# Sampling weights made by halves, one shift moved behind the samples, a later table load, and one neighbour tap instead of two

## Chip, core and metric

One NeuronCore of one Trainium2 chip runs the whole program; there is one launch and no other core takes part. The metric is device microseconds of one execution. Busy times below are per engine: PE is TensorE, PEld its weight loads, DVE is VectorE, ACT is ScalarE, POOL is GpSimd, SP is SyncE.

## What is computed

The input is 8 images of 32 channels and 16x16 pixels. Three layers follow one another: a deformable-attention block, plain self-attention over the 256 tokens of each image, and a routed feed-forward layer. The change lies in the first:

```
q   = wq x                                  (1x1 convolution of the normalised image)
off = w_off gelu(norm(depthwise 5x5, stride 4, of q))      -> 16 key points per image and group
pos = reference points + tanh(off[0:2]) / 4
xs  = bilinear sample of x at pos, times sigmoid(off[2])
k,v = wk xs, wv xs
bias[m, n] = bilinear sample of the table rpe at (query m - pos n)
out = softmax(q k * scale + bias) v,  x += wo out
```

There are G = 2 groups of 16 channels, each with 2 heads, and 16 keys a group and image. The hat of a distance d is max(0, 1 - |d|); a bilinear sample is a sum over all pixels or rows weighted by hats.

## The kernel before

Every engine has an instruction list written out by hand, in order, with explicit semaphores; no planner or scheduler moves anything. `link(...)` issues an instruction and makes its own engine wait until it has finished. Most tiles have 128 partitions: image times channel of a group, key of all images (8 x 16), or half of the 256 pixels.

What concerns the change, in the order of the data:

- **Hats of the samples.** ACT forms `a_smp` (|pixel - position|, slots 0 and 1 for the rows of the two halves of the image, slot 2 for the columns; L547) and `hat_smp` from all three slots in one instruction (L558). POOL multiplies slots 0 and 2, then 1 and 2, to `w_smp[:, 0]` and `w_smp[:, 1]` (L486).
- **Samples.** PE multiplies the transposed image by `w_smp` into `xs_ps` (L744), two halves for each of two groups, summed in PSUM. DVE multiplies by the sigmoid written as 1 + tanh(half) to `xs` (L1116). PE projects `xs` to keys (L754, `project(0)`), ACT copies them for each head to `kv` (L571).
- **Table of the bias.** PE interpolates rows of the table (L733) to `row_ps[g]`: 128 keys, 32 rows (16 image rows x 2 heads), 21 columns of which 17 or so are wanted, starting at a whole column shift of 0 to 4 that differs by key. DVE moves the columns in place with predicated copies (L1101): by 2 where `over[..., 1]`, by 1 where `over[..., 3]`, by 1 where `odd`; three copies for each group. What is left is a fraction of a column, and three products by `tap` (L390), with weights `tap_prev`, `tap_next`, `tap_here`: `left`, `right`, `here`. Group 0's are made by POOL from `win`, a copy in SBUF that ACT makes (L566); group 1's by DVE from PSUM.
- **Logits.** PE transposes each product, adding in PSUM, to `lg_ps` (L761, `turn_on`), and adds q k (L783), for half h = 0 and then 1 of the query pixels. `logits_done` lets DVE take the maximum (L1130) and subtract it (L1131); ACT makes the exponents (L577, L581). PE meanwhile projects values (L754 again), adds the image (L797) and multiplies by wo (L805); then it transposes the probabilities (L816).
- **Fillers.** `keep_busy` (L680) has PE multiply zeros, a fixed number of times, where it would otherwise stand: 20 ahead of L744, 8 ahead of the key projection.
- **Table of functions.** ACT loads the set with Ln and Exp (L511) behind `half_tanh` (L562) and ahead of `win`.

Of the kernel before, what the change touches and what calls it, by code (L numbers as in the profile page):

```python
# [14 lines left out]
P = 128  # L15
B, C = 8, 32
IMG = 16
# [113 lines left out]
def build(nc, x_in, consts_in, weights_in, w1_in, w2_in, out):  # L131
    with ExitStack() as ctx:
# [9 lines left out]
        def bank(n, cols=512):  # L142
            return ps[:, 512 * n:512 * n + cols]
# [143 lines left out]

        qpad_ps = [bank(2 + g, PADIMG * PADIMG).rearrange("p (y x) -> p y x", y=PADIMG) for g in range(G)]
# [134 lines left out]
        def _(pool):  # L423
            steps = [0]

            def link(ins):
                steps[0] += 1
                ins.then_inc(pool_step, 1)
                pool.wait_ge(pool_step, steps[0])
# [52 lines left out]
            nc.gpsimd.tensor_scalar(tap_next[:, :, :], dist[:, :, :], 0.0, None, ALU.max)  # L482
            link(nc.gpsimd.tensor_scalar(tap_prev[:, :, :], dist[:, :, :], -1.0, 0.0, ALU.mult, ALU.max))
            pool.wait_ge(hat_smp_ready, 1)
            for h in range(NHALF):
                nc.gpsimd.tensor_tensor(w_smp[:, h], hat_smp[:, h], hat_smp[:, 2], ALU.mult).then_inc(w_smp_ready, 1)  # L486
# [18 lines left out]
        def _(act):  # L505
# [38 lines left out]
            def distance(a, k, axis, place):  # L544

                act.wait_ge(points_ready, axis + 1)
                return nc.scalar.activation(a[:, k], points[:, axis], ACT.Abs, bias=const(place)[:, k:k + 1],  # L547
                                            scale=-1.0)
# [5 lines left out]
            for k in range(3):  # L554
                distance(a_smp, k, 0 if k < NHALF else 1, "at_pixel").then_inc(a_smp_ready, 1)

            act.wait_ge(a_smp_ready, 3)
            nc.scalar.activation(hat_smp[:, :, :], a_smp[:, :, :], ACT.Relu, bias=1.0, scale=-1.0).then_inc(  # L558
                hat_smp_ready, 1)
# [3 lines left out]
            load_table(LN_EXP_SET)  # L563

            act.wait_ge(shifts_done, 1)
            nc.scalar.activation(win[:, :, :], row_ps[0][:, :, 0:IMG + 1], ACT.Copy).then_inc(win_copied, 1)  # L566
# [103 lines left out]
        def _(pe):  # L670
            mm = nc.tensor.matmul

            def nx_rows(nx):

                return slice(nx * P // NK, (nx + 1) * P // NK)
# [53 lines left out]
            for g in range(G):  # L729
                for yq in range(4):  # L730
                    pe.wait_ge(hat_rel_ready, yq + 1)
                    for nx, least in enumerate(table_columns()[0]):
                        last = mm(row_ps[g][nx_rows(nx), 8 * yq:8 * yq + 8, 0:WIN],  # L733
                                  minus_hat_rel[:, yq, g * P + nx:(g + 1) * P:NK],
                                  rpe_blk[:, g].rearrange("p k (h c) -> p (k h) c", h=HG)[:, :, least:least + WIN],
                                  start=True, stop=True)
                last.then_inc(rows_done, 1)
# [3 lines left out]
            pe.wait_ge(w_smp_ready, 2)  # L741
            for g in range(G):
                for h in range(NHALF):
                    last = mm(xs_ps[:, g], xn_tok[:, h, g], w_smp[:, h, g * P:(g + 1) * P],  # L744
                              start=(h == 0), stop=(h == NHALF - 1))
# [23 lines left out]
            pe.wait_ge(txh_ready, 1)  # L769
            pe.wait_ge(part_ready[0], 1)  # L770
# [6 lines left out]
            pe.wait_ge(part_ready[1], 1)  # L777
            for h in range(NHALF):
                turn_on(left, 1, h)
            pe.wait_ge(k_ready, HG)  # L780
            for h in range(NHALF):
                for g in range(G):
                    mm(lg_ps[:, h, g].rearrange("p t k j -> p (t k j)"), q_sb[:, g, h * P:(h + 1) * P],  # L783
                       kv[:, 0, g].rearrange("p t k j -> p (t k j)"), start=False, stop=False, skip_group_check=True)
                pe.wait_ge(part_ready[1], 2)
                turn_on(right, 1, h)
                pe.wait_ge(part_ready[0], 3)
                turn_on(here, 0, h)
                pe.wait_ge(part_ready[1], 3)
                turn_on(here, 1, h).then_inc(logits_done, 1)  # L790
# [243 lines left out]
        def _(dve):  # L1034
# [64 lines left out]
            def shifted(g, width, mask, by):  # L1099

                return nc.vector.copy_predicated(  # L1101
                    row_ps[g][:, :, 0:width], mask.bitcast(U32).unsqueeze(2).to_broadcast([P, IMG * HG, width]),
                    row_ps[g][:, :, by:by + width])
# [9 lines left out]
            link(shifted(1, IMG + 2, over[:, 1, 3:4], 1))  # L1113
# [3 lines left out]
                in1=xs_ps.rearrange("p g n -> p (g n)"), op0=ALU.add, op1=ALU.mult).then_inc(xs_ready, 1)  # L1117
            shifted(1, IMG + 1, odd[:, 1:2], 1).then_inc(shifts_done, 1)
# [3 lines left out]
            dve.wait_ge(left_edge_zeroed, 1)  # L1122
            tap(nc.vector, left, 1, row_ps[1], -1, tap_prev, 1).then_inc(part_ready[1], 1)
            tap(nc.vector, right, 1, row_ps[1], 1, tap_next).then_inc(part_ready[1], 1)
            tap(nc.vector, here, 1, row_ps[1], 0, tap_here).then_inc(part_ready[1], 1)
# [165 lines left out]
```

## Time and profile before

| | |
|---|---|
| runs | 60.14, 60.37, 61.9 us; median 60.37 |
| profiled execution | 59.97 us, its span 58.0 us |
| PE busy | 50.6 us (87% of the span), fillers included |
| PEld, DVE, ACT, POOL busy | 41.8, 36.9, 29.9, 18.4 us |
| granted TensorE clock | 1.0 in all 40 slices of the span |
| chain that ended last | PE 57%, DVE 14%, POOL 8%, ACT 7%, issue 5%, DMA 4% |

The span runs from the first to the last instruction; 1.97 us of the profiled execution lie around it. The rows of a timeline give start, length, engine, line, operation, output and inputs, and in brackets how long the engine stood before and for whom. Times of neighbours on one engine overlap a little, because an instruction starts before the one ahead has drained.

### The profile page before, as it was taken

What the parts mean: (1) busy time and instruction counts of PE and PEld (TensorE: products, weight loads), DVE (VectorE), ACT (ScalarE), POOL (GpSimd) and SP (SyncE); (2) the same over time, 40 slices, a digit from 0 to 9 for tenths busy, and PEclk for the clock granted to TensorE, in tenths of its full rate; (3) what the DMA queues carried; (4) which work ended last, traced back from release to release, by engine and by line L of the source; (5) the groups of instructions that cost most, each with busy time, mean ns of one, the idle gap of its engine ahead of it and who ended that gap; (6) DMA issues with size and microseconds to landing.
All of it is one profiled execution on the core that took longest, in us unless ns stands there. A gap on an engine that the chain in (4) does not pass through costs nothing.

```text
span 58.0 us, 1496 instructions
## 1 busy us (share of the span) xinstructions
PE 50.6 (87%) x603; PEld 41.8 (72%) x603; DVE 36.9 (64%) x95; ACT 29.9 (52%) x66; POOL 18.4 (32%) x41
## 2 busy tenths in 40 slices
PE   3996996999699699999999999979999998979720
PEld 3995894985388579899898986726688675867500
DVE  3478399775659989449994046739267866785320
ACT  0802052787999903104744785197984639801020
POOL 6130089995878899910060000000000000000000
PEclk9999999999999999999999999999999999999999
DMA  0889931110000000000000000000000000000013
GB/s 0 206 183 263 253 105 46 57 41 11 0 0 0 0 11 0 0 0 0 0 0 0 0 0 17 6 0 0 0 0 11 0 0 0 0 0 0 0 44 136
DMA packets 3926, 2.02 MB, mean 35 GB/s; under 512 B 2640, under 2 KB 3792, under 8 KB 3920
## 3 DMA queue, kind: packets, MB, share of 16 engines
q1 hardware_dynamic: 1424, 1.37, 8.1%
q10 hardware_dynamic: 2496, 0.57, 4.7%
q8 instruction: 4, 0.07, 0.5%
q14 instruction: 2, 0.02, 0.1%
HBM read 1.67 MB, written 0.26 MB: 33 GB/s over the span
## 4 chain that ended last, share of the span: by engine, by line
PE 57%; DVE 14%; POOL 8%; ACT 7%; issue 5%; DMA 4%; DVEq 0%; ACTq 0%
PE ps L761 5%; DMA x_sb<-x_rows 4%; PE ps L805 4%; PE ps L754 4%; PE ps L826 4%; PE ps L680 3%; PE ps L884 3%; PE ps L867 3%; PE ps L783 3%; DVE taps L1070 3%; POOL w_smp L486 2%; PE ps L889 2%; ACT e_tok L621 2%; DVE off L1072 2%; PE ps L1030 2%
## 5 line engine op out<-in xcount | busy, mean ns | idle before, releaser
L680 PE MATMUL ps<-zeros 128*128 128x128 bf16 x145 | 11.2, 237 | 1.0 <-DVE zeros L1047 1.0
L680 PEld LDWEIGHTS ps<-zeros 128*128 128x128 bf16 x145 | 10.1, 107 | 1.5 <-DVE zeros L1047 1.0
L511 ACT ACT_TABLE_LOAD x4 | 5.1, 1283 | 1.7 <-PEq L1284 1.6
L621 ACT ACTIVATE e_tok<-ps,cst 128x512 f32<-128x512 f32 (+1 forms) x6 | 4.5, 828 | 1.5 <-PE ps L867 1.5
L1101 DVE COPY_PREDICATED ps<-over,ps 128x608 f32<-128x608 uint32 (+1 forms) x4 | 3.1, 777 | 0.8 <-PE ps L733 0.7
L733 PE MATMUL ps<-rpe_blk,minus_hat_rel 128*32 128x168 f32 x64 | 2.8, 316 | 0.5 <-DVE minus_hat_rel L1097 0.5
L571 ACT ACTIVATE kv<-ps,cst 128x256 f32<-128x256 f32 x4 | 1.7, 472 | 2.8 <-PE ps L754 2.8
L733 PEld LDWEIGHTS ps<-rpe_blk,minus_hat_rel 128*32 128x32 f32 x64 | 2.0, 142 | 1.3 <-issue 0.9
L884 PE MATMUL ps<-e_tok,t 128*32 128x128 f32 (+1 forms) x48 | 2.8, 310 | 0.0
L1148 DVE TENSOR_REDUCE ln_ss<-ln_sq 128x8 f32<-128x264 f32 x2 | 0.9, 428 | 3.0 <-ACT ln_sq L601 3.0
L867 PE MATMUL ps<-t_t 32*128 32x256 f32 x32 | 2.3, 398 | 0.4 <-ACT e_tok L621 0.4
L439 POOL TENSOR_TENSOR wblk<-wts,cst 128x256 f32<-128x256 f32 x3 | 1.9, 628 | 2.2 <-DMA wts<-weights 2.2
L398 POOL TENSOR_TENSOR d_prob<-d_exp,d_rec 128x512 f32<-128x512 f32 x1 | 1.1, 1058 | 4.6 <-DVE d_rec L1137 4.6
L1130 DVE TENSOR_REDUCE d_max<-ps 128x32 f32<-128x512 f32 x2 | 1.4, 692 | 1.7 <-PE ps L761 1.6
L577 ACT ACTIVATE d_exp<-d_sub 128x512 f32<-128x512 f32 x1 | 0.6, 629 | 3.4 <-DVE d_sub L1131 3.4
L690 PE MATMUL ps<-xn,wblk 128*128 128x256 f32 x8 | 2.0, 388 | 0.5 <-DVE xn L1063 0.5
L835 PE MATMUL ps<-prob_t,vo 128*128 128x256 f32 x8 | 2.3, 393 | 0.0
L754 PE MATMUL ps<-xs,wblk 128*128 128x128 f32 x16 | 2.2, 281 | 0.1
L527 ACT ACTIVATE xn_tok<-ps 128x512 f32<-128x512 f32 x1 | 0.6, 598 | 3.2 <-PE ps L697 3.2
L867 PEld LDWEIGHTS ps<-t_t 32*128 32x128 f32 x32 | 1.5, 184 | 0.9 <-issue 0.9
L754 PEld LDWEIGHTS ps<-xs,wblk 128*128 128x128 f32 x16 | 1.9, 191 | 0.3 <-DVE xs L1116 0.3
L1070 DVE TENSOR_TENSOR taps<-ps,wts 128x100 f32<-128x100 f32 x8 | 1.5, 253 | 1.0 <-PE ps L690 1.0
(189 smaller groups left out, 129.9 us busy)
## 6 DMA issues: line engine op xcount, KB each, us to landing
w_sb<-weight ACTq DMA_DIRECT2D x1, 256.0 KB, 6.0
w_sb<-weight SPq DMA_DIRECT2D x1, 256.0 KB, 5.2
x_nat<-x_rows SPq DMA_DIRECT2D x8, 32.0 KB
wts<-weights SPq DMA_DIRECT2D x1, 192.5 KB, 4.5
cst<-shape_consts SPq DMA_DIRECT2D x1, 192.0 KB, 4.1
x_sb<-x_rows SPq DMA_DIRECT2D x1, 128.0 KB, 2.4
x_sb<-x_rows ACTq DMA_DIRECT2D x1, 128.0 KB, 2.6
cst<-shape_consts SPq DMA_DIRECT2D x1, 128.0 KB, 5.0
```

Source lines behind the costliest of these rows:

```text
L511: nc.scalar.add_instruction(mybir.InstLoadActFuncSet(name=nc.get_next_instruction_name(), act_func_set_id=functions, ins=[], outs=[]))
L621: return nc.scalar.activation(dst, scores, ACT.Exp, bias=const("bound"))
L680: mm(bank(n_bank, P), zeros[:, :], zeros[:, :], start=True, stop=True)
L733: last = mm(row_ps[g][nx_rows(nx), 8 * yq:8 * yq + 8, 0:WIN], minus_hat_rel[:, yq, g * P + nx:(g + 1) * P:NK], rpe_blk[:, g].rearrange("p ...
L754: last = mm(kv_ps[w][:, g], wblk[:, 1 + w, gi, g].rearrange("p b o -> p (b o)"), xs[:, gi], start=(gi == 0), stop=(gi == G - 1))
L761: last = mm(lg_ps[:, h, g, :, hh], part[:, g, hh, 8 * h:8 * h + 8].rearrange("p y x -> p (y x)"), back_to_n[:, :].rearrange("p (t j) -> p ...
L805: last = mm(outputs[:, g, t], kv[:, 1, g, t].rearrange("p k j -> p (k j)"), blk[:, g, B4 * t:B4 * t + B4].rearrange("p b o -> p (b o)"), s ...
L826: last = mm(att_ps[h][:, P * t:P * t + P], prob_t[:, h, g, t], vo_c[:, g, t], start=False, stop=(g == G - 1), skip_group_check=True)
L867: return mm(scores, t1_t[rows, b // B4, h * P:(h + 1) * P], t1_t[rows, b // B4, :], start=start, stop=True, skip_group_check=True)
L884: return mm(out[C * (b % B4):C * (b % B4) + C], t1[:, h, b], e_tok[:, b, h, queries], start=start, stop=stop, skip_group_check=True)
L1070: last = tt(taps[:, g, i].rearrange("p j (a b) -> p j a b", a=KS), conv_view(g, i), dw, ALU.mult)
L1101: return nc.vector.copy_predicated(row_ps[g][:, :, 0:width], mask.bitcast(U32).unsqueeze(2).to_broadcast([P, IMG * HG, width]), row_ps[g][ ...
```

## The change

1. ACT makes the hats one by one: distance of the columns, of half 0's rows, their two hats, then distance and hat of half 1. POOL makes `w_smp` half by half as the hats come, ahead of `tap_prev` instead of behind it. PE waits for one half at a time and takes half 0 of both groups first.
2. DVE makes `xs` between the first and the second shift of group 1, not between the second and third.
3. ACT copies `win` before it loads the set with Exp.
4. The table rows stand one column further right in `row_ps` (column 0 is free); `table_ps` is the view from column 1. For group 1, DVE makes `here` first; then a predicated copy overwrites each column by the one two further right where `tap_next` is not zero, so that the column holds the right neighbour for one sign of the fraction and the left for the other; then one product with `tap_both` (the sum of the two weights, of which one is zero) takes the place of `left` and `right`. PE has four transposes fewer, and adds q k before group 1's parts.

```diff
--- before.py
+++ after.py
@@ -285,6 +285,7 @@
         sq_ps = [bank(n, M) for n in (4, 2)]
         y_ps = [bank(n, M) for n in (1, 5)]
 
+        table_ps = [row_ps[g][:, :, 1:] for g in range(G)]
         qpad_ps = [bank(2 + g, PADIMG * PADIMG).rearrange("p (y x) -> p y x", y=PADIMG) for g in range(G)]
         q_ps = [qpad_ps[g][:, PAD:PAD + IMG, PAD:PAD + IMG] for g in range(G)]
         att_ps = [bank(2 + h, B * C) for h in range(NHALF)]
@@ -480,10 +481,10 @@
             link(nc.gpsimd.tensor_tensor(dist[:, :, :], frac[:, :].unsqueeze(2).to_broadcast([P, G, IMG]),
                                          const("frac_x").unsqueeze(1).to_broadcast([P, G, IMG]), ALU.subtract))
             nc.gpsimd.tensor_scalar(tap_next[:, :, :], dist[:, :, :], 0.0, None, ALU.max)
+            for h in range(NHALF):
+                pool.wait_ge(hat_smp_ready, 2 + h)
+                nc.gpsimd.tensor_tensor(w_smp[:, h], hat_smp[:, h], hat_smp[:, 2], ALU.mult).then_inc(w_smp_ready, 1)
             link(nc.gpsimd.tensor_scalar(tap_prev[:, :, :], dist[:, :, :], -1.0, 0.0, ALU.mult, ALU.max))
-            pool.wait_ge(hat_smp_ready, 1)
-            for h in range(NHALF):
-                nc.gpsimd.tensor_tensor(w_smp[:, h], hat_smp[:, h], hat_smp[:, 2], ALU.mult).then_inc(w_smp_ready, 1)
             link(nc.gpsimd.tensor_tensor(tap_both[:, :, :], tap_next[:, :, :], tap_prev[:, :, :], ALU.add))
             nc.gpsimd.tensor_scalar(tap_here[:, :, :], tap_both[:, :, :], -1.0, 1.0, ALU.mult,
                                     ALU.add).then_inc(taps_ready, 1)
@@ -551,19 +552,24 @@
             for k in range(4):
                 distance(a_rel, k, 0, "at_row").then_inc(a_rel_ready, 1)
 
-            for k in range(3):
-                distance(a_smp, k, 0 if k < NHALF else 1, "at_pixel").then_inc(a_smp_ready, 1)
-
-            act.wait_ge(a_smp_ready, 3)
-            nc.scalar.activation(hat_smp[:, :, :], a_smp[:, :, :], ACT.Relu, bias=1.0, scale=-1.0).then_inc(
-                hat_smp_ready, 1)
+            def hat(k, after):
+
+                act.wait_ge(a_smp_ready, after)
+                return nc.scalar.activation(hat_smp[:, k], a_smp[:, k], ACT.Relu, bias=1.0, scale=-1.0)
+
+            distance(a_smp, 2, 1, "at_pixel").then_inc(a_smp_ready, 1)
+            distance(a_smp, 0, 0, "at_pixel").then_inc(a_smp_ready, 1)
+            hat(2, 1).then_inc(hat_smp_ready, 1)
+            hat(0, 2).then_inc(hat_smp_ready, 1)
+            distance(a_smp, 1, 0, "at_pixel").then_inc(a_smp_ready, 1)
+            hat(1, 3).then_inc(hat_smp_ready, 1)
 
             act.wait_ge(off_done, 4)
             nc.scalar.activation(half_tanh[:, :], off_ps[2], ACT.Tanh, scale=0.5).then_inc(half_tanh_ready, 1)
+
+            act.wait_ge(shifts_done, 1)
+            nc.scalar.activation(win[:, :, :], table_ps[0][:, :, 0:IMG + 1], ACT.Copy).then_inc(win_copied, 1)
             load_table(LN_EXP_SET)
-
-            act.wait_ge(shifts_done, 1)
-            nc.scalar.activation(win[:, :, :], row_ps[0][:, :, 0:IMG + 1], ACT.Copy).then_inc(win_copied, 1)
 
             def copy_heads(w, ready):
 
@@ -730,7 +736,7 @@
                 for yq in range(4):
                     pe.wait_ge(hat_rel_ready, yq + 1)
                     for nx, least in enumerate(table_columns()[0]):
-                        last = mm(row_ps[g][nx_rows(nx), 8 * yq:8 * yq + 8, 0:WIN],
+                        last = mm(row_ps[g][nx_rows(nx), 8 * yq:8 * yq + 8, 1:1 + WIN],
                                   minus_hat_rel[:, yq, g * P + nx:(g + 1) * P:NK],
                                   rpe_blk[:, g].rearrange("p k (h c) -> p (k h) c", h=HG)[:, :, least:least + WIN],
                                   start=True, stop=True)
@@ -738,11 +744,11 @@
             keep_busy("w_smp_ready", 5)
 
             pe.wait_ge(half_tanh_ready, 1)
-            pe.wait_ge(w_smp_ready, 2)
-            for g in range(G):
-                for h in range(NHALF):
+            for h in range(NHALF):
+                pe.wait_ge(w_smp_ready, h + 1)
+                for g in range(G):
                     last = mm(xs_ps[:, g], xn_tok[:, h, g], w_smp[:, h, g * P:(g + 1) * P],
-                              start=(h == 0), stop=(h == NHALF - 1))
+                              start=(h == 0 and g == 0), stop=(h == NHALF - 1), skip_group_check=True)
             last.then_inc(sampled, 1)
             keep_busy("xs_ready", 6)
             pe.wait_ge(xs_ready, 1)
@@ -767,6 +773,7 @@
 
             pe.wait_ge(back_to_n_ready, 1)
             pe.wait_ge(txh_ready, 1)
+            pe.wait_ge(left_edge_zeroed, 1)
             pe.wait_ge(part_ready[0], 1)
             for h in range(NHALF):
                 turn_on(left, 0, h, start=True)
@@ -774,20 +781,24 @@
             for h in range(NHALF):
                 turn_on(right, 0, h)
 
-            pe.wait_ge(part_ready[1], 1)
-            for h in range(NHALF):
-                turn_on(left, 1, h)
-            pe.wait_ge(k_ready, HG)
-            for h in range(NHALF):
+            def by_keys(h):
+
                 for g in range(G):
                     mm(lg_ps[:, h, g].rearrange("p t k j -> p (t k j)"), q_sb[:, g, h * P:(h + 1) * P],
                        kv[:, 0, g].rearrange("p t k j -> p (t k j)"), start=False, stop=False, skip_group_check=True)
-                pe.wait_ge(part_ready[1], 2)
-                turn_on(right, 1, h)
-                pe.wait_ge(part_ready[0], 3)
-                turn_on(here, 0, h)
-                pe.wait_ge(part_ready[1], 3)
-                turn_on(here, 1, h).then_inc(logits_done, 1)
+
+            pe.wait_ge(k_ready, HG)
+            by_keys(0)
+            pe.wait_ge(part_ready[1], 1)
+            turn_on(here, 1, 0)
+            pe.wait_ge(part_ready[0], 3)
+            turn_on(here, 0, 0)
+            pe.wait_ge(part_ready[1], 2)
+            turn_on(right, 1, 0).then_inc(logits_done, 1)
+            turn_on(here, 1, 1)
+            by_keys(1)
+            turn_on(here, 0, 1)
+            turn_on(right, 1, 1).then_inc(logits_done, 1)
 
             project(1).then_inc(v_done, 1)
             pe.wait_ge(x_nat_loaded, 16 * B)
@@ -1099,8 +1110,8 @@
             def shifted(g, width, mask, by):
 
                 return nc.vector.copy_predicated(
-                    row_ps[g][:, :, 0:width], mask.bitcast(U32).unsqueeze(2).to_broadcast([P, IMG * HG, width]),
-                    row_ps[g][:, :, by:by + width])
+                    table_ps[g][:, :, 0:width], mask.bitcast(U32).unsqueeze(2).to_broadcast([P, IMG * HG, width]),
+                    table_ps[g][:, :, by:by + width])
 
             dve.wait_ge(masks_ready, 1)
             dve.wait_ge(rows_done, 1)
@@ -1110,19 +1121,21 @@
 
             dve.wait_ge(rows_done, 2)
             link(shifted(1, IMG + 3, over[:, 1, 1:2], 2))
-            link(shifted(1, IMG + 2, over[:, 1, 3:4], 1))
             dve.wait_ge(sampled, 1)
             dve.wait_ge(half_tanh_ready, 1)
             stt(out=xs[:, :, :].rearrange("p g n -> p (g n)"), in0=half_tanh[:, :], scalar=1.0,
                 in1=xs_ps.rearrange("p g n -> p (g n)"), op0=ALU.add, op1=ALU.mult).then_inc(xs_ready, 1)
+            link(shifted(1, IMG + 2, over[:, 1, 3:4], 1))
             shifted(1, IMG + 1, odd[:, 1:2], 1).then_inc(shifts_done, 1)
 
             dve.wait_ge(shifts_done, 2)
             dve.wait_ge(taps_ready, 1)
-            dve.wait_ge(left_edge_zeroed, 1)
-            tap(nc.vector, left, 1, row_ps[1], -1, tap_prev, 1).then_inc(part_ready[1], 1)
-            tap(nc.vector, right, 1, row_ps[1], 1, tap_next).then_inc(part_ready[1], 1)
-            tap(nc.vector, here, 1, row_ps[1], 0, tap_here).then_inc(part_ready[1], 1)
+            tap(nc.vector, here, 1, table_ps[1], 0, tap_here).then_inc(part_ready[1], 1)
+            dve.wait_ge(part_ready[1], 1)
+            link(nc.vector.copy_predicated(
+                row_ps[1][:, :, 0:IMG], tap_next[:, 1].bitcast(U32).unsqueeze(1).to_broadcast([P, IMG * HG, IMG]),
+                row_ps[1][:, :, 2:IMG + 2]))
+            tap(nc.vector, right, 1, row_ps[1], 0, tap_both).then_inc(part_ready[1], 1)
 
             lg_rows = [lg_ps[:, h].rearrange("p g t k (b n) -> p (g t k b) n", n=N) for h in range(NHALF)]
             for h in range(NHALF):
```

On PE, from the fillers ahead of the samples to the value projection, before (`ps` is PSUM; `left`, `right`, `here` are the products of the taps):

```order
L744 MATMUL ps<-w_smp,xn_tok 128x128 x4
L680 MATMUL ps<-zeros 128x128 x8
L754 MATMUL ps<-xs,wblk 128x128 x4
L761 MATMUL ps<-back_to_n,left 128x2x64 x4
L761 MATMUL ps<-back_to_n,right 128x2x64 x4
L761 MATMUL ps<-back_to_n,left 128x2x64 x4
L783 MATMUL ps<-kv,q_sb 128x256 x2
L761 MATMUL ps<-back_to_n,right 128x2x64 x2
L761 MATMUL ps<-back_to_n,here 128x2x64 x4
L783 MATMUL ps<-kv,q_sb 128x256 x2
L761 MATMUL ps<-back_to_n,right 128x2x64 x2
L761 MATMUL ps<-back_to_n,here 128x2x64 x4
```

The same place with the change:

```order
L750 MATMUL ps<-w_smp,xn_tok 128x128 x4
L686 MATMUL ps<-zeros 128x128 x8
L760 MATMUL ps<-xs,wblk 128x128 x4
L767 MATMUL ps<-back_to_n,left 128x2x64 x4
L767 MATMUL ps<-back_to_n,right 128x2x64 x4
L787 MATMUL ps<-kv,q_sb 128x256 x2
L767 MATMUL ps<-back_to_n,here 128x2x64 x4
L767 MATMUL ps<-back_to_n,right 128x2x64 x2
L767 MATMUL ps<-back_to_n,here 128x2x64 x2
L787 MATMUL ps<-kv,q_sb 128x256 x2
L767 MATMUL ps<-back_to_n,here 128x2x64 x2
L767 MATMUL ps<-back_to_n,right 128x2x64 x2
```

The second group of four `left` transposes is gone, q k of half 0 stands where they stood, and `right` of group 1 is the last part of each half.

On DVE, from group 1's first shift to the first maximum, before:

```order
L1101 COPY_PREDICATED ps<-over,ps 128x32x19
L1101 COPY_PREDICATED ps<-over,ps 128x32x18
L1116 SCALAR_TENSOR_TENSOR xs<-half_tanh,ps 128x256
L1101 COPY_PREDICATED ps<-odd,ps 128x32x17
L390 TENSOR_TENSOR left<-ps,tap_prev 128x32x15
L390 TENSOR_TENSOR right<-ps,tap_next 128x512
L390 TENSOR_TENSOR here<-ps,tap_here 128x512
L1130 TENSOR_REDUCE d_max<-ps 128x32
```

With the change:

```order
L1112 COPY_PREDICATED ps<-over,ps 128x32x19
L1126 SCALAR_TENSOR_TENSOR xs<-half_tanh,ps 128x256
L1112 COPY_PREDICATED ps<-over,ps 128x32x18
L1112 COPY_PREDICATED ps<-odd,ps 128x32x17
L391 TENSOR_TENSOR here<-ps,tap_here 128x512
L1135 COPY_PREDICATED ps<-tap_next,ps 128x32x16
L391 TENSOR_TENSOR right<-ps,tap_both 128x512
L1143 TENSOR_REDUCE d_max<-ps 128x32
```

The number of instructions is the same; one more of them stands behind `xs`, and the last product now hangs on a copy in front of it.

On ACT, from the distances of the samples to the key copies, with the change (before, it was three `a_smp`, one `hat_smp` of 128x768, `half_tanh`, the load, `win`):

```order
L548 ACTIVATE a_smp<-points,cst 128x256 x2
L558 ACTIVATE hat_smp<-a_smp 128x256 x2
L548 ACTIVATE a_smp<-points,cst 128x256
L558 ACTIVATE hat_smp<-a_smp 128x256
L568 ACTIVATE half_tanh<-ps 128x256
L571 ACTIVATE win<-ps 128x544
L512 ACT_TABLE_LOAD
L577 ACTIVATE kv<-ps,cst 128x4x64 x2
```

Two hats more are issued, and the load has moved from ahead of `win` to behind it.

## Rows read from the trace of the kernel before

**Rows 1.** The chain of waits: start us, us, engine, what it works on.
```profile
11.00 1.56 PE ps L680 x28
...
18.20 1.42 POOL w_smp L486 x2
...
19.76 1.14 PE ps L744 x8
...
20.98 0.43 DVE xs L1116
...
21.46 1.16 PE ps L754 x8
```
**Rows 2.** The timeline of POOL.
```profile
17.42 0.29 POOL L482 TENSOR_SCALAR tap_next<-dist 128x32 f32<-128x32 f32 x1
17.78 0.33 POOL L483 TENSOR_SCALAR tap_prev<-dist 128x32 f32<-128x32 f32 x1
...
19.57 0.25 POOL L487 TENSOR_TENSOR tap_both<-tap_next,tap_prev 128x32 f32<-128x32 f32 x1
19.91 0.22 POOL L488 TENSOR_SCALAR tap_here<-tap_both 128x32 f32<-128x32 f32 x1
20.28 1.15 POOL L390 TENSOR_TENSOR left<-win,tap_prev 128x480 f32<-128x480 f32 x1 [0.15 <-ACT win L566]
21.39 1.20 POOL L390 TENSOR_TENSOR right<-win,tap_next 128x512 f32<-128x512 f32 x1
22.54 1.22 POOL L390 TENSOR_TENSOR here<-win,tap_here 128x512 f32<-128x512 f32 x1
```
**Rows 3.** The timeline of ACT.
```profile
15.82 1.29 ACT L547 ACTIVATE a_smp<-points,cst 128x256 f32<-128x256 f32 x3
17.14 0.85 ACT L558 ACTIVATE hat_smp<-a_smp 128x768 f32<-128x768 f32 x1
17.90 0.36 ACT L562 ACTIVATE half_tanh<-ps 128x256 f32<-128x256 f32 x1
18.28 1.28 ACT L511 ACT_TABLE_LOAD   x1
19.57 0.62 ACT L566 ACTIVATE win<-ps 128x544 f32<-128x544 f32 x1
22.65 0.84 ACT L571 ACTIVATE kv<-ps,cst 128x256 f32<-128x256 f32 x2 [2.45 <-PE ps L754]
```
**Rows 4.** The timeline of DVE.
```profile
18.58 0.73 DVE L1101 COPY_PREDICATED ps<-odd,ps 128x544 f32<-128x544 uint32 x1
19.22 1.58 DVE L1101 COPY_PREDICATED ps<-over,ps 128x608 f32<-128x608 uint32 x2
...
21.32 0.72 DVE L1101 COPY_PREDICATED ps<-odd,ps 128x544 f32<-128x544 uint32 x1
22.07 0.66 DVE L390 TENSOR_TENSOR left<-ps,tap_prev 128x480 f32<-128x480 f32 x1
...
23.25 0.68 DVE L390 TENSOR_TENSOR here<-ps,tap_here 128x512 f32<-128x512 f32 x1
25.48 0.69 DVE L1130 TENSOR_REDUCE d_max<-ps 128x32 f32<-128x512 f32 x1 [1.56 <-PE ps L761]
```
**Rows 5.** The timeline of PE.
```profile
17.90 1.29 PE L680 MATMUL ps<-zeros 128*128 128x128 bf16 x20
...
22.45 0.60 PE L761 MATMUL ps<-back_to_n,left 128*128 128x128 f32 x4
22.89 0.60 PE L761 MATMUL ps<-back_to_n,right 128*128 128x128 f32 x4
...
23.76 1.03 PE L783 MATMUL ps<-kv,q_sb 128*128 128x256 f32 x4
24.63 0.38 PE L761 MATMUL ps<-back_to_n,right 128*128 128x128 f32 x2
...
26.80 1.06 PE L754 MATMUL ps<-xs,wblk 128*128 128x128 f32 x8
```
**Rows 6.** One line's instructions (L1101): ns min/median/max, first and last start, forms.
```profile
L1101 DVE COPY_PREDICATED ps<-over,ps x4: 761/776/797, 17.0 to 20.0; 128x608 f32<-128x608 uint32 x2, 128x576 f32<-128x576 uint32 x2
```

## Prediction

> **What bounds it now.** I read the chain of waits first, because busy shares average over stages: PE is busy 87% of the span, but part of that is fillers. Through the stage that the change touches the chain runs POOL `w_smp`, PE samples, DVE `xs`, PE key projection [rows 1], and from there PE without a gap to the value projection [rows 5]. So two things can shorten it: `xs` earlier, and less work on PE between 22.45 and 26.80. Then I read the timelines of POOL, ACT and DVE [rows 2 to 4] for what arrives at PE just in time and will be late when PE comes sooner. Behind the logits DVE stands 1.56 us for PE before its first maximum [rows 4], ACT and PE follow from there, and nothing that they need comes from a fixed earlier time (the key copies of ACT wait 2.45 us for PE [rows 3]); so I take what the logits gain as the gain of the end.
>
> **Part 1, hats and samples.** ACT: three distances cost 1.29 us, 0.40 from start to start, and the hat of 768 columns 0.85; a copy of 544 columns takes 0.62 and one of 256 (x2) 0.84 [rows 3]. A hat of 256 is then about 0.42 alone and 0.33 behind another. From 15.82: distances until 16.71, hat of the columns from 16.62, hat of half 0 done at 17.37, distance of half 1 done at 17.77, its hat at 18.22, `half_tanh` at 18.49 instead of 18.26. That is 0.23 us more on ACT; it is hidden, since `win` has to wait for the third shift of group 0 until 19.31 (18.58 + 0.73, [rows 4]).
>
> POOL: `tap_next` ends at 17.71 and half 0's hats are there, so `w_smp` starts at 17.66 where it started at 18.20; two take 1.42 [rows 1, 2] and end at 19.08. Half 1's hat (18.22) is there before its product needs it at 18.35. PE, however, has 20 fillers from 17.90 [rows 5]. 28 such go in 1.56 us [rows 1], so 20 take 1.11 and the samples can start at 19.05, not before. Half 0 lasts about 0.5, and half 1 is wanted at 19.55 with its weights there since 19.2. So samples start at 19.05 for 19.76: **0.71 us earlier, by fillers and no longer by POOL**. They take 1.14 and end at 20.19; DVE has then just ended the first shift of group 1 (19.22 + 0.80 = 20.02 [rows 4, 6]). `xs` starts at 20.27 for 20.98 and the key projection at 20.75 for 21.46.
>
> **Part 2, the order on DVE.** From `xs` on: `xs` 0.42, of which the next instruction waits 0.34 (20.98 to 21.32, [rows 1, 4]); second shift 0.76 (the smaller form, [rows 6]) and 0.03 for its link; third 0.72; `here` starts 0.75 behind the third's start (21.32 to 22.07). So: second shift 20.61, third 21.40, `here` 22.15 to 22.83.
>
> The new predicated copy is in no row. Above, 608, 576 and 544 columns cost 797, 761 and 725 ns [rows 4, 6]: 36 ns for 32 columns, so 512 cost 0.69. Its mask runs along the columns instead of standing still for a row. The lower bound is 0.66 (the tap of 480, [rows 4]), the upper 1.22, which POOL needs for 512 [rows 2]; nothing suggests that it could cost less than a plain tap. I take 0.69, as it is the same instruction in the same memory. `right` then takes 0.68. With 0.04 at each of two links: copy 22.87 to 23.56, `right` 23.59 to 24.27. Before, DVE was done at 23.93 [rows 4]; now it ends 0.34 later, although it started 0.71 earlier.
>
> **Part 3, `win` and the load.** `win` starts at 19.33 for 19.57 and ends at 19.96. POOL, behind `w_smp` at 19.08, makes `tap_prev`, `tap_both`, `tap_here` by 20.00 (0.33, 0.25, 0.22 and links of 0.07 to 0.09, [rows 2]), so `left` of group 0 starts at 20.06 for 20.28, `right` ends at 22.37, `here` at 23.54. The load of 1.28 us [rows 3] now runs from 19.96 to 21.24. The key copies are wanted at 21.94, so it costs nothing: its cover is 0.7 us of standing. `win` started 0.01 us behind the load's end [rows 3], so I book 1.28 and no more.
>
> The Trainium skill says otherwise (*ScalarE: Activation LUTs*, What ACT_TABLE_LOAD costs): 1283 ns of load and about 1380 ns of drain, some 2.66 us for every switch. By that page the key copies would start at about 22.6 and the sum below would lose about 0.5 us.
>
> **Part 4, PE.** Keys projected 20.75 to 21.90, four `left` transposes from 21.74 to 22.18 (0.44 for four: 22.45 to 22.89, [rows 5]). Then the path meets POOL: `right` of group 0 is done at 22.37 and its transposes start at 22.43, a stand of 0.25. They end at 22.87; q k of half 0 takes 0.87 (23.76 to 24.63, [rows 5]) with its copies done at 22.78; 23.74. `here` of group 1 and then of group 0, 0.22 each: 24.18, both ready. `right` of group 1 is ready at 24.27 and starts at 24.33: 0.15 of standing, now on DVE's chain. Half 0 is issued by 24.55; half 1 needs 0.22 + 0.87 + 0.22 + 0.22 = 1.53 and ends at 26.08. Before it was 26.80 [rows 5].
>
> **Sum.** 0.71 (samples earlier) + 0.44 (four transposes gone) - 0.25 - 0.15 (PE stands for POOL, then for DVE) = 0.75; by the times, 26.80 - 26.08 = 0.72. I take 0.7. The profiled execution, 59.97 us, becomes 59.3; it lies 0.4 below the median 60.37, and on the scale of the median the time is **59.7 us**, 1.2% less. The bounds of the copy make it 59.6 to 60.2.
>
> **Rivals.**
>
> *A. The stands vanish.* If POOL's and DVE's products come 0.25 and 0.15 sooner (the copy runs beside nothing, say, and POOL's taps start straight behind `w_smp`), the gain is 0.71 + 0.44 = 1.15 us: 59.2. For it: both stands are small. Against it: POOL's three products take 1.15 to 1.22 in a row and are bound by `win`. A gain over 2% (1.2 us; 2% is about what a measurement of this kernel can tell from no change) needs some 0.05 us more. Chance 0.14.
>
> *B. DVE's chain takes it all.* Six dependent instructions stand between the samples and the last part of half 0, where five stood and three parts came singly. If the copy costs POOL's 1.22 us, PE stands 0.53 more and the gain is 0.2; if it reads its mask as a second stream and doubles to 1.38, the gain is nil: 59.9 to 60.4. The same comes out if the samples do not start earlier, that is, if the half-by-half hats do not do what they say: `xs` at 20.98 puts the last part at 24.98 and the gain at 0.05. Against it: mask and data already come from two memories at full rate [rows 6]. Chance 0.20.
>
> *C. The load is longer than its row once keys wait for it.* Were ACT held another 1.28 us behind it, key copies would run from 22.52 to 23.36 instead of to 22.78, q k would start 0.5 later, and of that 0.15 is DVE's stand anyway: gain 0.35, 60.0. The page cited above would have it so; the row shows `win` straight behind the load. Chance 0.04.
>
> *D. Slower.* The copy pays its fixed part anew for each of the 32 rows of the table. From the three forms the fixed part is 725 - 544 x 1.125 = 113 ns; 32 of them are 3.6 us in place of 0.11, its price is 4.2 us, and the end moves by 3.5 - 0.7 = 2.8 us: 63.2. It decides from 1.4 us for the copy on. For it: no row has a mask that changes within a row and comes back for the next. Against it: the shifts have the same 32 rows and show no such part. Chance 0.03.
>
> **Numbers.** The forecast has 0.59. The rivals in order have 0.14, 0.20, 0.04 and 0.03. A and the scatter of three runs, whose lowest was 0.23 under the median, give the low end, 59.1; B gives the high end, 60.4; outside lie D, part of A and disturbed medians. Faster by over 2%: 0.15, which is A's upper part with scatter on the forecast. Slower by over 2%: 0.04. Within 2%: 0.81.
>
> **What the changed profile would show.** Samples on PE straight behind the fillers, at about 19.05, released by no one; `xs` at 20.3; the new copy near 0.69 us; PE standing about 0.25 for POOL's `right` and 0.15 for DVE's `right`; the first maximum at 24.8 for 25.48, the value projection at 26.1 for 26.80; key copies without a wait for the load. If the copy's row is over 1 us, or the second group of samples waits for `w_smp`, parts 2 or 1 are wrong. If the logits gain 0.7 but the span does not, something behind them is bound by a time of its own, which I excluded from ACT's and DVE's standing alone.

## The result

| | before | changed | ratio of the runs, 95% interval |
|---|---|---|---|
| first comparison | 60.47 us median of 8 (lowest 59.91) | 60.62 us median of 8 (lowest 59.38) | 0.9884 [0.9842, 0.9926] |
| second series of runs | 60.61 us median of 11 (lowest 60.39) | 59.53 us median of 6 (lowest 59.34) | 0.9829 [0.9801, 0.9857] |

The change makes the kernel 1.2 to 1.7% faster, 0.7 to 1.0 us, less than 2%. The medians of the first row say little, since 4 of its 8 runs of the changed kernel were disturbed (61.2 to 61.5 us; in three of them the mean granted clock of TensorE was 0.963 to 0.975) and the ratios leave such runs out; the median of the other four is 59.64 us.

So that executions with different starts can be compared, I use one **stage time** below: from the start of ACT's first tanh to the start of the value projection on PE. Before it is 26.80 - 13.33 = **13.47 us**. In every trace below the granted clock is 1.0 throughout this stage.

### The profile page after: what moved, and what is told of

Read it like the earlier page. It is cut to its first block, busy times and chain, and to the rows that moved or that the text cites. A ratio compares the mean times of both kernels' runs of the same rounds, so it can differ in the third digit from the quotient of the medians.

```text
span 59.1 us, 1490 instructions
## 1 busy us (share of the span) xinstructions
PE 52.4 (89%) x599; PEld 42.9 (72%) x599; DVE 37.0 (63%) x95; ACT 30.1 (51%) x68; POOL 18.4 (31%) x41
## 2 busy tenths in 40 slices
DMA packets 3926, 2.02 MB, mean 34 GB/s; under 512 B 2640, under 2 KB 3792, under 8 KB 3920
## 4 chain that ended last, share of the span: by engine, by line
PE 61%; POOL 12%; DVE 11%; ACT 7%; issue 4%; DVEq 0%; ACTq 0%; POOLq 0%
PE ps L686 12%; PE ps L816 3%; PE ps L837 3%; PE ps L767 3%; PE ps L1041 3%; PE ps L895 3%; PE ps L878 3%; PE ps L787 3%; PE ps L696 3%; DVE taps L1081 2%; PE ps L900 2%; POOL w_smp L486 2%; ACT e_tok L627 2%; POOL right L391 2%; DVE off L1083 2%
## 5 line engine op out<-in xcount | busy, mean ns | idle before, releaser
L686 PE MATMUL ps<-zeros 128*128 128x128 bf16 x145 | 12.1, 248 | 1.0 <-DVE zeros L1058 1.0
L686 PEld LDWEIGHTS ps<-zeros 128*128 128x128 bf16 x145 | 10.9, 114 | 1.5 <-DVE zeros L1058 1.0
L696 PE MATMUL ps<-xn,wblk 128*128 128x256 f32 x8 | 2.5, 468 | 0.0
L1041 PE MATMUL ps<-chosen,out_blk 128*128 128x256 f32 x4 | 1.9, 640 | 0.4 <-DVE out_blk L1253 0.4
L696 PEld LDWEIGHTS ps<-xn,wblk 128*128 128x128 f32 x8 | 1.9, 247 | 0.4 <-issue 0.2
```

The source lines that it names most:

```text
L686: mm(bank(n_bank, P), zeros[:, :], zeros[:, :], start=True, stop=True)
L696: last = mm(q_ps[g], wblk[:, 0, gi, g].rearrange("p b o -> p (b o)"), xn[:, gi].rearrange("p (y x) -> p y x", y=IMG), start=(gi == 0), sto ...
L1041: mm(y_ps[t], out2_blk[:, B4 * t:B4 * t + B4].rearrange("p b o -> p (b o)"), chosen[:, :], start=(t == 0), stop=True, skip_group_check=Tru ...
```

## The profile after

The first profiled execution of the changed kernel took longer (span 59.1 us) than the second (57.5 us) for two reasons, both outside the stage. This is its page, the clock by slices:

```profile
PEclk9999999999999999999999999999999999999555
```

and this its PE timeline at the end, the last product of the program:

```profile
54.61 1.95 PE L1041 MATMUL ps<-chosen,out_blk 128*128 128x256 f32 x4 [0.42 <-DVE out_blk L1253]
```

In the second profiled execution (span 57.5 us) the same row is

```profile
53.82 1.13 PE L1041 MATMUL ps<-chosen,out_blk 128*128 128x256 f32 x4 [0.42 <-DVE out_blk L1253]
```

The last three slices ran at the lower of the clock's two levels, and the product took 0.8 us more. The other 0.8 us come ahead of the stage: the first tanh starts at 14.21 us in the first execution and at 13.41 in the second. The rows from here on are of the second execution. The chain of waits through the stage:

```profile
17.49 0.29 POOL tap_next L483
17.78 1.37 POOL w_smp L486 x2
19.15 0.09 issue
19.24 0.35 POOL tap_prev L487
...
19.66 0.26 POOL tap_both L488
...
20.00 0.23 POOL tap_here L489
...
20.37 1.15 POOL left L391
21.52 1.18 POOL right L391
22.70 0.04 issue
22.74 0.66 PE ps L767 x4
```

Before, the chain left POOL after `w_smp` and ran over samples, `xs` and the key projection [rows 1]. Now it stays on POOL through the taps and two products, and reaches PE only at the transposes of `right`. PE's timeline:

```profile
17.98 1.29 PE L686 MATMUL ps<-zeros 128*128 128x128 bf16 x20
19.11 1.11 PE L750 MATMUL ps<-w_smp,xn_tok 128*128 128x128 f32 x8
...
20.79 1.16 PE L760 MATMUL ps<-xs,wblk 128*128 128x128 f32 x8
21.79 0.60 PE L767 MATMUL ps<-back_to_n,left 128*128 128x128 f32 x4
22.74 0.66 PE L767 MATMUL ps<-back_to_n,right 128*128 128x128 f32 x4 [0.36 <-POOL right L391]
23.23 1.03 PE L787 MATMUL ps<-kv,q_sb 128*128 128x256 f32 x4
24.10 0.60 PE L767 MATMUL ps<-back_to_n,here 128*128 128x128 f32 x4
24.54 0.38 PE L767 MATMUL ps<-back_to_n,right 128*128 128x128 f32 x2
...
26.27 1.06 PE L760 MATMUL ps<-xs,wblk 128*128 128x128 f32 x8
```

Against [rows 5]: the samples follow the fillers with no stand; `left` and the rest are 0.7 earlier; then there is a stand for POOL (four transposes take 0.44 of PE's time, so PE is free at 22.23 and starts at 22.74, a stand of 0.51; the 0.36 in brackets counts from the end of the row before, 22.39), and none ahead of the last `right`. The stage time is 26.27 - 13.41 = **12.86 us**, 0.61 less. DVE, to be held against [rows 4]:

```profile
20.32 0.42 DVE L1126 SCALAR_TENSOR_TENSOR xs<-half_tanh,ps 128x256 f32<-128x256 f32 x1 [0.22 <-DVE ps L1112]
...
22.21 0.69 DVE L391 TENSOR_TENSOR here<-ps,tap_here 128x512 f32<-128x512 f32 x1
22.93 0.69 DVE L1135 COPY_PREDICATED ps<-tap_next,ps 128x512 f32<-128x512 uint32 x1
23.66 0.69 DVE L391 TENSOR_TENSOR right<-ps,tap_both 128x512 f32<-128x512 f32 x1
24.95 0.69 DVE L1143 TENSOR_REDUCE d_max<-ps 128x32 f32<-128x512 f32 x1 [0.60 <-PE ps L767]
```

The new copy costs 0.69 us, and DVE's last product ends at 24.35, 0.19 before PE takes it. ACT, against [rows 3]:

```profile
18.16 0.36 ACT L568 ACTIVATE half_tanh<-ps 128x256 f32<-128x256 f32 x1
19.43 0.62 ACT L571 ACTIVATE win<-ps 128x544 f32<-128x544 f32 x1 [0.90 <-DVE ps L1112]
20.07 1.28 ACT L512 ACT_TABLE_LOAD   x1
21.99 0.84 ACT L577 ACTIVATE kv<-ps,cst 128x256 f32<-128x256 f32 x2 [0.63 <-PE ps L760]
```

The key copies wait for PE, 0.64 us behind the end of the load.

## The experiments

All are judged by the stage time, and by the ratio to the kernel before in the same series of runs. A ratio is known here to between 0.3 and 0.5%, 0.2 to 0.3 us; the stage time told apart far less, since the same program gave 12.87 and 12.86 in two executions.

| kernel | stage time us | ratio to before [95%] |
|---|---|---|
| before | 13.47 | 1 |
| changed | 12.87, 12.86 | 0.9884, 0.9829 (above) |
| taps_only | 13.35 | 0.9971 [0.9926, 1.0016] |
| halves_only | 13.30 | 0.9958 [0.9916, 1.0001] |
| hats_whole | 13.34 | 0.9948 [0.9896, 1.0001] |
| load_first | 13.04 | 0.9888 [0.9847, 0.9929] |
| xs_late | 13.21 | one run, not compared |
| act_taps | 12.79 | 0.9832 [0.9786, 0.9878] |
| v_half | 12.87 | 0.9817 [0.9791, 0.9843] |
| fill14 | 12.86 | 0.984 [0.9787, 0.9894] |
| act_taps_fill14 | 12.68 | 0.9798 [0.9754, 0.9842] |

**The changed kernel again.**

> The changed kernel once more, beside the experiments of this call: both theories expect the ratio on record, 0.988, and 12.87 us from the first tanh to the value projection.

The ratio came out at 0.9829, whose interval does not hold 0.988, but overlaps that of the first comparison. The stage time was as expected.

**Do the parts add up?** First the tap by sign alone, on hats, samples and order of before (table at column 1 kept):

```diff
-            distance(a_smp, 2, 1, "at_pixel").then_inc(a_smp_ready, 1)
...
+            act.wait_ge(a_smp_ready, 3)
+            nc.scalar.activation(hat_smp[:, :, :], a_smp[:, :, :], ACT.Relu, bias=1.0, scale=-1.0)...
...
+            load_table(LN_EXP_SET)
             act.wait_ge(shifts_done, 1)
```

> Only part 4 of the change on the kernel before: group 1's neighbour tap by sign, four transposes fewer; hats, samples, order of xs and the load as before. Measure: from the start of the first tanh to the start of the value projection, 13.47 us before (13.33 to 26.80) and 12.87 with the whole change (14.21 to 27.08). Theory (the parts hide each other's gains; what PE takes next has to be there): xs as before, PE saves 0.44 but then stands 0.2 for the key copies, which end at 23.49 on the clock of before; 13.24, gain 0.23. Rival (the parts add up, each gives its own term): gain 0.44, 13.03.

Its PE timeline:

```profile
22.62 0.60 PE L762 MATMUL ps<-back_to_n,left 128*128 128x128 f32 x4
23.06 0.60 PE L762 MATMUL ps<-back_to_n,right 128*128 128x128 f32 x4
23.72 1.13 PE L782 MATMUL ps<-kv,q_sb 128*128 128x256 f32 x4
```

No stand ahead of `right`, but one of 0.2 for the key copies (ACT's end at 22.83 + 0.84 = 23.67): 13.35, a gain of 0.12. The theory had 0.23, the additive rival 0.44; the products behind the stand also took 0.96 to the next row's start instead of 0.87, which the theory lacked.

Then the other parts alone, with three taps on DVE and PE's old order:

```diff
+            dve.wait_ge(left_edge_zeroed, 1)
+            tap(nc.vector, left, 1, table_ps[1], -1, tap_prev, 1).then_inc(part_ready[1], 1)
+            tap(nc.vector, right, 1, table_ps[1], 1, tap_next).then_inc(part_ready[1], 1)
             tap(nc.vector, here, 1, table_ps[1], 0, tap_here).then_inc(part_ready[1], 1)
-            dve.wait_ge(part_ready[1], 1)
-            link(nc.vector.copy_predicated(...))
-            tap(nc.vector, right, 1, row_ps[1], 0, tap_both).then_inc(part_ready[1], 1)
```

> Parts 1 to 3 without part 4: hats by halves, xs between the shifts, load behind win, but group 1 with its three taps and the order on PE of before. Theory (POOL's product right of group 0 times PE): samples 0.7 earlier, PE stands 0.5 for POOL ahead of right of group 0, gain 0.16, 13.31 from the first tanh to the value projection. Rival (additive): gain 0.7, 12.77.

```profile
20.75 1.16 PE L760 MATMUL ps<-xs,wblk 128*128 128x128 f32 x8
21.75 0.60 PE L767 MATMUL ps<-back_to_n,left 128*128 128x128 f32 x4
22.71 0.66 PE L767 MATMUL ps<-back_to_n,right 128*128 128x128 f32 x4 [0.36 <-POOL right L391]
```

13.30, where the theory had 13.31 and the additive rival 12.77: samples come 0.7 earlier, and 0.52 of it is a stand for POOL. Alone the parts are worth 0.12 and 0.17 us, together 0.61. **The transposes need the early `xs`:** without it they run into the key copies, which costs the stand of 0.22 and 0.09 for the slower products behind it, 0.31 together; that is the 0.32 by which the whole exceeds the two parts. POOL's stand explains none of this difference, since it is as long with the saved transposes (0.51) as without them (0.52); it eats most of what the early `xs` brings in either case.

**What the hats by halves are for.**

```diff
-            hat(2, 1).then_inc(hat_smp_ready, 1)
-            hat(0, 2).then_inc(hat_smp_ready, 1)
...
+            act.wait_ge(a_smp_ready, 3)
+            nc.scalar.activation(hat_smp[:, :, :], a_smp[:, :, :], ACT.Relu, bias=1.0, scale=-1.0)...
```

> The changed kernel with one hat instruction for all three slots, as before; POOL's order, PE's waits and all else as changed. Theory (the half-by-half hats count because POOL gets to its taps and products sooner, not because the samples start sooner): w_smp starts 0.37 later, xs only 0.05 later since fillers hold the samples anyway, left and right of group 0 0.37 later, and PE stands that much longer ahead of right; 13.2 against 12.87. Rival (samples are what counts): 12.9.

13.34, a loss of 0.47; the theory had 0.33 and the rival 0.03. POOL's timeline:

```profile
18.46 1.41 POOL L486 TENSOR_TENSOR w_smp<-hat_smp 128x256 f32<-128x256 f32 x2 [0.43 <-ACT hat_smp L559]
...
21.09 1.15 POOL L391 TENSOR_TENSOR left<-win,tap_prev 128x480 f32<-128x480 f32 x1
```

Counted from the first tanh (13.66 here), `w_smp` starts at 4.80 instead of 4.33 (0.47 later, where 0.37 was expected), `left` at 7.43 instead of 6.96 and `xs` at 7.07 instead of 6.91. The stage loses what POOL loses, 0.47, not what `xs` loses, 0.16. The halves pay by sending POOL to its taps earlier.

**The load.**

```diff
+            load_table(LN_EXP_SET)
             act.wait_ge(shifts_done, 1)
             nc.scalar.activation(win[:, :, :], ...).then_inc(win_copied, 1)
-            load_table(LN_EXP_SET)
```

> The changed kernel with the load of the Exp set ahead of win again. Theory: the load runs 18.5 to 19.8 on the clock of before, win ends 0.45 later, and left of group 0, which waits for the taps until 20.30 anyway, starts 0.2 later, at 20.49; PE stands 0.2 longer: 13.07 against 12.87. Rival (POOL is bound by its taps alone, or the load costs more when keys wait for it in the changed order): no difference, or faster than 12.87.

```profile
19.27 1.28 ACT L512 ACT_TABLE_LOAD   x1
20.56 0.62 ACT L572 ACTIVATE win<-ps 128x544 f32<-128x544 f32 x1
```

13.04, 0.17 lost, as the theory had it. The two timed ratios do not show that, being 0.9888 here and 0.9884 in the first comparison; the trace does.

**The order of `xs`.**

```diff
+            link(shifted(1, IMG + 2, over[:, 1, 3:4], 1))
             dve.wait_ge(sampled, 1)
...
-            link(shifted(1, IMG + 2, over[:, 1, 3:4], 1))
```

> The changed kernel with xs behind group 1's second shift, as before. Theory (PE stands for POOL anyway): xs and the key projection 0.57 later, the stand of 0.5 ahead of right of group 0 goes, but the key copies then come late and PE stands 0.2 for them; 13.1. Rival (additive): 0.57 lost in full, 13.44.

```profile
23.04 0.60 PE L767 MATMUL ps<-back_to_n,right 128*128 128x128 f32 x4
23.70 1.13 PE L787 MATMUL ps<-kv,q_sb 128*128 128x256 f32 x4
24.66 0.60 PE L767 MATMUL ps<-back_to_n,here 128*128 128x128 f32 x4
```

13.21: `xs` 0.60 later, 0.35 lost. The stand for POOL went and one of 0.22 for the key copies came (23.04 + 0.44 to 23.70), as with taps_only; the products behind it again took 0.96, which the theory lacked. Its 13.1 is nearer than 13.44. The time of the whole run, 61.69 us, is long for a reason behind the stage: the last output transfer took 3.6 us where it took 1.7 to 1.8 in all other traces but load_first's (3.1).

**Is it POOL's chain, and what holds it?**

```diff
+            nc.scalar.activation(tap_both[:, :, :], dist[:, :, :], ACT.Abs).then_inc(both_ready, 1)
+            act.wait_ge(both_ready, 1)
+            nc.scalar.activation(tap_here[:, :, :], tap_both[:, :, :], ACT.Relu, bias=1.0, scale=-1.0)...
             act.wait_ge(shifts_done, 1)
...
-            link(nc.gpsimd.tensor_tensor(tap_both[:, :, :], tap_next[:, :, :], tap_prev[:, :, :], ALU.add))
-            nc.gpsimd.tensor_scalar(tap_here[:, :, :], tap_both[:, :, :], -1.0, 1.0, ALU.mult, ...)
```

> The changed kernel with tap_both and tap_here made by ACT (the magnitude of dist, then 1 minus it, two small instructions ahead of win, where ACT stands 0.9 us) instead of by POOL behind w_smp. Theory (POOL's chain taps, left, right of group 0 times PE now): left starts 0.25 earlier, bound by win, PE stands 0.25 less ahead of right, and then 0.1 for DVE's right of group 1; 12.73 us from the first tanh to the value projection, gain 0.14 over the changed kernel. Rival (left is bound by win already in the changed kernel, as I had it in the prediction): 12.87, no gain.

Its POOL and PE timelines:

```profile
20.37 1.15 POOL L392 TENSOR_TENSOR left<-win,tap_prev 128x480 f32<-128x480 f32 x1 [0.59 <-POOL tap_prev L490]
```

```profile
22.74 0.66 PE L773 MATMUL ps<-back_to_n,right 128*128 128x128 f32 x4 [0.17 <-POOL right L392]
...
24.10 0.60 PE L773 MATMUL ps<-back_to_n,here 128*128 128x128 f32 x4
24.59 0.44 PE L773 MATMUL ps<-back_to_n,right 128*128 128x128 f32 x2
```

From the first tanh (13.60) `left` starts at 6.77, 0.19 earlier where 0.25 was expected, so its taps did hold it. The bracket names `tap_prev`, but that ended at 19.78; what `left` now waits for is `win`, which ended at 20.23. PE gains 0.19 ahead of `right` and gives 0.11 back to DVE's `right`: PE could have started its transposes at 24.54 (24.10 + 0.44) and started at 24.59, and the two took 0.28 instead of 0.22. That makes 12.79, a gain of 0.07 where 0.14 was expected.

**Fewer fillers**, 20 to 14, on the changed kernel and on act_taps:

```diff
-    ... "w_smp_ready": 20, "xs_ready": 8,
+    ... "w_smp_ready": 14, "xs_ready": 8,
```

> The changed kernel with 14 fillers instead of 20 ahead of the samples. In the changed kernel the samples start straight behind the fillers. Theory (fillers hold xs, but POOL's right of group 0 times PE): samples start 0.33 earlier and wait for half 1's weights, xs starts 0.2 earlier, straight behind DVE's first shift of group 1 (6.7 us after the first tanh instead of 6.9), and PE stands 0.2 longer ahead of right; value projection unchanged at 12.86. Rival (an earlier xs is worth its size, as in my sum): 12.66.

> ACT makes tap_both and tap_here, and 14 fillers: the version that the experiments point to. Theory: with POOL 0.19 earlier, PE stood 0.1 for DVE's right of group 1; with xs 0.2 earlier that goes too, 12.68 from the first tanh to the value projection, 0.18 less than the changed kernel and 0.1 less than act_taps; ratio to before about 0.98, which one call of runs can hardly tell from the changed kernel's. Rival (additive, 0.2 + 0.19 in full): 12.47.

`xs` on DVE with 14 fillers alone, and PE's transposes with ACT's taps as well:

```profile
20.35 0.42 DVE L1126 SCALAR_TENSOR_TENSOR xs<-half_tanh,ps 128x256 f32<-128x256 f32 x1
```

```profile
21.96 0.60 PE L773 MATMUL ps<-back_to_n,left 128*128 128x128 f32 x4
22.92 0.66 PE L773 MATMUL ps<-back_to_n,right 128*128 128x128 f32 x4 [0.36 <-POOL right L392]
```

Both stage times came out to the hundredth: with 14 fillers alone `xs` starts 6.71 after the first tanh for 6.91 and the stage takes 12.86 as in the changed kernel; with ACT's taps it takes 12.68. An earlier `xs` is worth nothing while POOL's `right` is last, and 0.11 once POOL is 0.19 earlier. The last kernel has the lowest ratio of all, 0.9798 [0.9754, 0.9842]; its interval still overlaps that of the changed kernel, so that it beats it is shown by the trace and not by the times.

**Behind the logits.** PE's stand for POOL, 0.5 us, filled with half of the value projection:

```diff
                 turn_on(left, 0, h, start=True)
+            project(1, [0])
             pe.wait_ge(part_ready[0], 2)
...
-            project(1).then_inc(v_done, 1)
+            project(1, [1]).then_inc(v_done, 1)
```

> The changed kernel with group 0's half of the value projection put into PE's stand ahead of right of group 0 (0.45 us of work into 0.5 us). Measure: from the first tanh to the transposes of the probabilities, 16.74 us in the changed kernel. Theory (behind the logits DVE's softmax of both halves is as late as PE, so PE's saving is worth little): second half of the value projection starts at 12.9, woblk_c products 0.45 earlier, but d_prob is not earlier and PE stands for it; end of the transposes of the probabilities 0.0 to 0.1 earlier. Rival (PE is the bound behind the logits): 0.45 earlier, total 59.0.

```profile
22.45 0.61 PE L760 MATMUL ps<-xs,wblk 128*128 128x128 f32 x4
22.98 0.66 PE L767 MATMUL ps<-back_to_n,right 128*128 128x128 f32 x4
...
26.52 0.61 PE L760 MATMUL ps<-xs,wblk 128*128 128x128 f32 x4
30.30 1.20 PE L828 MATMUL ps<-cst,d_prob 128*128 128x128 f32 x8 [0.20 <-POOL d_prob L399]
31.34 0.33 PE L686 MATMUL ps<-zeros 128*128 128x128 bf16 x3
```

The filler ahead of the attention starts 17.69 after the first tanh (31.34 - 13.65); in the changed kernel 17.70 (31.11 - 13.41). PE saved 0.44 us and got nothing: its transposes of the probabilities start only 0.09 earlier (16.65 for 16.74), because it now stands for the probabilities of half 0, and they end at the same time. Behind the logits the softmax on DVE, ACT and POOL is as late as PE.

## Why the prediction was right, and where it was off

The time lies in the range (59.64 us in the first comparison, for 59.7), and the gain, 0.7 us forecast, was 0.61 in the stage and 0.70 and 1.03 by the two ratios (1.16% and 1.71% of 60.5). That the first ratio meets the forecast to the hundredth is luck: the stage, which is all that the forecast was about, gained 0.61. Times below count from the first tanh; 13.33 is taken off the prediction's.

- **Part 1, samples.** `w_smp` at 4.33 expected, 4.33 measured; samples 5.72 and 5.70; `xs` 6.94 and 6.91; key projection 7.42 and 7.38. Fillers, not POOL, hold the samples now: in fill14 they start at 5.35. The reason why the halves matter was incomplete. I booked 0.71 for `xs` and treated POOL as a deduction; hats_whole shows that the stage follows POOL.
- **Part 2, DVE.** Copy 0.69 expected and 0.69 measured; last product ends at 10.94 and 10.94. Rivals B and D fall with that row, and B's other way (samples no earlier) with the samples at 5.70.
- **Part 3, POOL's chain: the step that was mis-sized.** `left` of group 0 was to start at 6.73 and started at 6.96. Two gaps were missing. I let `tap_prev` start 0.04 before the end of `w_smp`, as `tap_both` had done; it starts 0.09 behind it. And I let `left` start 0.06 behind `tap_here`; it starts 0.15 behind (20.22 to 20.37). The second could be read in the rows of before: `tap_here` ends at 20.13, `left` starts at 20.28 [rows 2]. The row says that it waited for `win`, which came at 20.19; with the same 0.15 behind `tap_here` its own taps would have held it to the same moment. That `left` is held by its taps in the changed kernel, act_taps shows.
- **Part 3, the load.** Hidden, as booked: 1.28 us, and `win` 0.01 us behind it in load_first. The Trainium skill (*ScalarE: Activation LUTs*, What ACT_TABLE_LOAD costs) adds about 1380 ns of drain, with which the key copies could not have started before 22.7; they started at 21.99. The trace disagrees with that as a cost behind the load, and it shows none ahead of it either (`win` ends at 20.05, the load starts at 20.07); rival C falls.
- **Part 4, the stands.** Expected 0.25 for POOL and 0.15 for DVE, 0.40 in all. Measured: 0.51 for POOL, 0.05 more for the four transposes behind it (0.49 for 0.44), none for DVE. The larger first stand covers the second. That is 0.16 more than booked; the key projection, 0.04 earlier than booked, gives a part of it back, hence 0.61 and not the 0.72 that the times gave.
- **The end follows the logits.** True here: from the value projection to ACT's last copy 28.70 us before (26.80 to 55.50) and 28.71 after (26.27 to 54.98). But I gave only PE as the path behind; v_half shows that the softmax is level with it: 0.44 us saved on PE alone behind the logits were lost.
- **Rival A** needs both stands gone. DVE's did not come in the changed kernel (0.05 us in act_taps). POOL's is in every version that starts `xs` early: in act_taps_fill14, where POOL's product and `xs` both come 0.2 earlier, PE still stands 0.52 for it (21.96 + 0.44 to 22.92), and the gain over the changed kernel is 0.18.

**Open.** The second ratio says 1.03 us [0.87, 1.20], the trace of the same kernel 0.61. The times and spans of the runs behind that ratio say where most of the rest lies. The mean span fell from 58.41 to 57.68 us, 0.73, which is near the 0.61 of the stage, as spans are given to 0.1 us. The other 0.30 lie outside the span, before the first or behind the last instruction: 2.11 us before and 1.81 with the change (all these are means over the runs that the ratios use). The kernel before has 2.10 to 2.11 in all three series of experiments, and every experiment with more than one run that holds part 4 has 1.80 to 1.82, halves_only, without part 4, 2.02; the changed kernel in the first comparison has 1.89. What lies there no view shows, and its cause stays open. In taps_only and hats_whole these 0.3 us are the whole gain that their ratios have, with spans that do not differ from the span before by 0.02 us, so these two ratios do not confirm the gains of 0.12 and 0.13 in the stage. The first tanh starts between 13.33 and 14.21 us in the profiled executions, 13.33 in the only one of before; the warming fillers at the start took 4.10 us there and 4.98 and 4.61 in those of the changed kernel. That scatter lies within the spans. No run puts `tap_prev` back ahead of `w_smp` in the changed kernel, so what POOL's new order is worth by itself was not measured.

## What to carry to other kernels

When two inputs of an engine arrive within a few tenths of each other, size both chains before crediting either; the parts of a change can be worth 0.12 and 0.17 us alone and 0.61 together. A wait names only what came last: if a second condition was met 0.06 us before, removing the first buys at most that, and here nothing. Look for work to move off the engine whose chain is last (here two tiny POOL instructions to an idle ACT), and do not count work saved on an engine until the next one's chain has been laid beside it.

## What the runs showed of the hardware

- On POOL a TENSOR_SCALAR starts 0.07 to 0.09 us behind the end of the instruction ahead even without a wait between them (`tap_next` to `tap_prev` [rows 2]; `w_smp` to `tap_prev`, 19.15 to 19.24), while a TENSOR_TENSOR starts up to 0.04 before that end (`tap_next`, 17.78, to `w_smp`, 17.74). So it is for every such pair looked at in these traces, and an order of instructions has a price of its own there.
- A predicated copy whose mask runs along the columns and repeats for each of 32 rows costs what one with a mask standing still costs: 695 ns for 512 columns, 6 ns above the line through 797, 761 and 725 ns for 608, 576 and 544 [rows 6].
- PE's first instructions behind a stand cost 0.05 to 0.1 us more than the same ones in a stream: four transposes 0.49 for 0.44, four products of 256 columns 0.96 for 0.87 in taps_only and xs_late.
